# Attention with features: row tiles for the scores, early division of the probabilities, column tiles for the values

## The reference

```python
def _feature_map(x, fm_w, fm_b):
    z = jnp.einsum('nshd,ed->nshe', x, fm_w) + fm_b
    return jnp.concatenate([jnp.exp(z), jnp.exp(-z)], axis=-1)
v, k, q = (_feature_map(x, fm_w, fm_b) for x in (v, k, q))   # 16 heads of 16 -> 32 features
scores = jnp.einsum('nqhd,nkhd->nhqk', q, k) / jnp.sqrt(jnp.float32(EMBED))
attn = jax.nn.softmax(scores, axis=-1)
out = jnp.einsum('nhql,nlhd->nqhd', attn, v)
return out.reshape(N, S, HEADS * EXP_DIM) @ fc_w.T + fc_b
```

## Time and profile before

| | us |
|---|---|
| median of three runs | 1918.85 |
| the profiled execution, its own time | 1920.63 |
| its span | 1918.6 |
| the block that is rewritten (561.9 to 690.3) | 128.4 |
| mean granted clock, share of 2.4 GHz | 0.925 |

### The profile page before, as it was taken

One profiled execution on the slowest core, in us unless ns is written; L12 is line 12 of the kernel. 1 busy time (PEld: TensorE's weight loads), 2 busy tenths in 40 slices (PEclk: granted clock), 3 DMA queues, 4 the chain that ended last, 5 costly groups with the idle time before them and its releaser, 6 DMA issues. The chain is left out here.

```text
span 1918.6 us, 33572 instructions
## 1 busy us (share of the span) xinstructions
PE 1612.3 (84%) x11474; PEld 1174.2 (61%) x11506; DVE 980.2 (51%) x2463; ACT 459.2 (24%) x1027; POOL 399.2 (21%) x651
## 2 busy tenths in 40 slices
PE   4888999999879959699979899376997697999980
PEld 2664888888649943355544555254665463899970
DVE  5454344444476667666646233547885456222223
ACT  1331110111224421355621121242222231111000
POOL 2002111111250001111202343601221201222216
PEclk9999999999889979899989999558998899999995
DMA  3205988989410005334215122300000001899984
GB/s 113 56 2 163 307 298 296 296 303 288 146 55 1 0 1 140 102 99 111 74 30 160 43 82 75 93 6 1 0 0 1 1 2 45 289 322 317 311 251 134
DMA packets 163103, 240.39 MB, mean 125 GB/s; under 512 B 20032, under 2 KB 110464, under 8 KB 162880
## 3 DMA queue, kind: packets, MB, share of 16 engines
q1 hardware_dynamic: 152832, 211.34, 34.3%
q0 software_dynamic: 10176, 27.80, 5.5%
HBM read 208.93 MB, written 30.15 MB: 125 GB/s over the span
## 5 line engine op out<-in xcount | busy, mean ns | idle before, releaser
L1340 DVE TENSOR_REDUCE l1a_nm<-l1a_sc 128x1 f32<-128x512 f32 (+3 forms) x256 | 107.2, 482 | 53.7 <-PE l1a_sc L1476 53.7
L2070 PE MATMUL e0b_gp<-e0b_xT,e0b_wgu 128*128 128x128 f32 x936 | 114.9, 279 | 1.8 <-DVE e0b_hT L2140 1.3
L2070 PEld LDWEIGHTS e0b_gp<-e0b_xT,e0b_wgu 128*128 128x128 f32 x936 | 107.4, 192 | 14.5 <-issue 12.3
L2091 PE MATMUL e0b_yp<-e0b_wd,e0b_hT 128*128 128x256 f32 x468 | 115.1, 388 | 0.6 <-issue 0.6
L2121 ACT ACTIVATE e0b_sg<-e0b_gp 128x640 f32<-128x640 f32 x78 | 33.5, 481 | 285.0 <-PE e0b_gp L2070 285.0
L2091 PEld LDWEIGHTS e0b_yp<-e0b_wd,e0b_hT 128*128 128x128 f32 x468 | 82.6, 189 | 21.9 <-issue 13.9
L2070 PE MATMUL e0b_up<-e0b_xT,e0b_wgu 128*128 128x128 f32 x780 | 93.5, 275 | 0.0
L2070 PEld LDWEIGHTS e0b_up<-e0b_xT,e0b_wgu 128*128 128x128 f32 x780 | 90.2, 192 | 0.0
L2070 PE MATMUL e3b_gp<-e3b_xT,e3b_wgu 128*128 128x128 f32 x624 | 77.4, 277 | 10.1 <-DMA e3b_wgu<-in_L_ffn_W 9.5
L2070 PEld LDWEIGHTS e3b_gp<-e3b_xT,e3b_wgu 128*128 128x128 f32 x624 | 74.5, 192 | 16.5 <-DMA e3b_wgu<-in_L_ffn_W 9.7
L2225 PE MATMUL e1b_gu<-e_kgu,e1b_xT 128*128 x152 | 75.2, 617 | 4.4 <-DVE e1b_xT L2290 2.8
(11 more groups left out here) (576 smaller groups left out, 3566.8 us busy)
## 6 DMA issues: line engine op xcount, KB each, us to landing
e3b_wgu<-in_L_ffn_W SPq DMA_DIRECT2D x78, 512.0 KB, 5.5
e0b_wgu<-in_L_ffn_gate_proj SPq DMA_DIRECT2D x39, 704.0 KB, 4.6
e0b_wgu<-in_L_ffn_up_proj SPq DMA_DIRECT2D x39, 704.0 KB, 6.0
e0b_wd<-in_L_ffn_down_proj SPq DMA_DIRECT2D x39, 640.0 KB, 5.2
e3b_wd<-in_L_ffn_W SPq DMA_DIRECT2D x39, 512.0 KB, 6.6
x_rows<-xn SPq DMA_DIRECT2D x3, 2048.0 KB, 8.6
l_parts<-l1p_split SPq DMA_DIRECT2D x16, 384.0 KB, 3.1
l_stack_k<-l_parts SPq DMA_DIRECT2D x48, 128.0 KB, 2.8
```

Of the source, the lines that this page charges most:

```text
L1340: nc.vector.tensor_reduce(nm[:, g % 2, q, i:i + 1], sc[q], AX_X, ALU.max, negate=True).then_inc(max_done, 1)
L2070: last = nc.tensor.matmul(dst[:, f, :], wgu[j][:, k, at + f * P:at + (f + 1) * P], xT[j][:, k, :], start=(k == 0), stop=(k == KC - 1))
L2091: last = nc.tensor.matmul(yp[:], hT[j][0:FW[f], f, :], wd[j][0:FW[f], f, :], start=(f == 0), stop=(f == FC - 1))
```

## The change

The second block of `feature_attention` is written anew, and the layouts around it follow.

- The features are ordered so that 64 rows hold 2 heads (2 x 2 signs x 16). `fm_signs` is made by quarters of 32, `kd` holds two heads for each half of the rows (`side` in place of `head4`), and `scores` makes two products over 64 rows and 128 columns in place of one over 128 and 256: upper rows into bank `sc[0]`, lower into `sc[1]`.
- `sc` is one tile for all t, no longer two in turn; the transposed probabilities have banks of their own, `pt`.
- Maximum, subtraction and exponentials are done by halves of 8 heads, and `scale` multiplies the probabilities with the reciprocal, by halves, ahead of their transposition. `pr` has AHEAD = 3 buffers.
- `values` has 32 columns of `vd` as the stationary operand and the turned probabilities as the moving one: four products, for four heads, on four column tiles of the array, into the four quarters of the partitions of `ob`. The outputs arise turned; `turn_outputs`, `divide` and `ho` go.
- The bias comes as a product of one row into `yb`; GpSimd's addition goes.
- `w.fc1` is laid out for the new order of heads by eight loads in place of one.
- All loops are written out over t, each queue in an order of its own.

```diff
-    w.fc1, w.bo1 = matrix("L1_xattn_fc_wT", 2 * D, D), spread("L1_xattn_fc_b", D)
+    w.fc1, w.bo1 = sb("w_L1_xattn_fc_wT", [P, 2 * KC, D]), spread("L1_xattn_fc_b", D)
+    for c in range(2 * KC):
+        for half in range(2):
+            at = (c % 2 * 8 + half * 4 + c // 2 * 2) * 2 * HD
+            loads.append((w.fc1[half * P // 2:(half + 1) * P // 2, c, :], ins["L1_xattn_fc_wT"][at:at + P // 2, :]))
...
-                for half, sign in ((slice(0, P // 2), 1.0), (slice(P // 2, P), -1.0)):
+                for quarter in range(4):
+                    rows = slice(quarter * 2 * HD, (quarter + 1) * 2 * HD)
+                    sign = (1.0, -1.0)[quarter % 2]
                     for u in range(2):
-                        nc.vector.tensor_scalar(w.fm_signs[:, u, half], w.fm[:, u * P // 2:(u + 1) * P // 2], sign, None, ALU.mult)
-                    nc.vector.tensor_scalar(w.fmb_signs[half, :], w.fmb[half, :], sign, None, ALU.mult).then_inc(prep, 1)
+                        at = u * P // 2 + quarter // 2 * 2 * HD
+                        nc.vector.tensor_scalar(w.fm_signs[:, u, rows], w.fm[:, at:at + 2 * HD], sign, None, ALU.mult)
+                    nc.vector.tensor_scalar(w.fmb_signs[rows, :], w.fmb[rows, :], sign, None, ALU.mult).then_inc(prep, 1)
...
-                        nc.vector.tensor_tensor(kd[:, b, g], bcast(kT[:, g, b, :], 1, HQ), bcast(const("head4"), 2, L), ALU.mult)
+                        nc.vector.tensor_tensor(kd[:, b, g], bcast(kT[:, g, b, :], 1, 2), bcast(const("side"), 2, L), ALU.mult)
...
+            sc, pt, ob = ([ps(f"{n}{j}", s) for j in range(2)] for n, s in (
+                ("sc", [P, H // 2, L]), ("pt", [P, PAIRS // 2, P]), ("ob", [P, OC, P])))
...
-                    nc.gpsimd.tensor_tensor(x[:], x[:], bcast(bo[:], 1, T), ALU.add).then_inc(biased, 1)
...
+                    def scores(t):
                         pe.wait_ge(q_done, t + 1)
+                        if t >= 1:
+                            pe.wait_ge(less_done, t * 2)
                         for g in range(QC):
+                            for half in range(2):
+                                rows = slice(half * P // 2, (half + 1) * P // 2)
+                                last = nc.tensor.matmul(sc[half][:, g * 2:g * 2 + 2, :].rearrange("p h l -> p (h l)"),
+                                                        qT[rows, t % 2, g, :], kd[rows, t // TB, g].rearrange("p a l -> p (a l)"),
+                                                        start=True, stop=True)
+                                if g == QC - 1:
+                                    last.then_inc(sc_made, 1)
+                    def turn_probs(t):
+                        for half in range(2):
+                            pe.wait_ge(pr_done, t * 2 + half + 1)
+                            if t >= 1:
+                                pe.wait_ge(pt_half, t * 2 + half - 1)
+                            for r in range(half * 4, half * 4 + 4):
+                                last = nc.tensor.transpose(pt[half][:, r % 4, :],
+                                                           pr[t % AHEAD][:, 2 * r:2 * r + 2, :].rearrange("p h l -> p (h l)"), ident)
+                            last.then_inc(pt_made, 1)
+                    def values(t):
+                        if t >= 2:
+                            pe.wait_ge(ot_done, t - 1)
                         for c in range(OC):
+                            if c % 2 == 0:
+                                pe.wait_ge(pt_half, t * 2 + c // 2 + 1)
+                            for i in range(4):
+                                r, a = c * 2 + i // 2, i % 2
+                                pair = r % 4 * 2 + r // 4
+                                last = nc.tensor.matmul(ob[t % 2][i * VD:(i + 1) * VD, c, :], vd[:, t // TB, pair, a, :], pT[:, r, :],
+                                                        start=True, stop=True)
+                        last.then_inc(o_made, 1)
                     def project(t):
...
+                        nc.tensor.matmul(yb[:], ones[0:1, :], bo[0:1, :], start=True, stop=False)
                         for c in range(OC):
+                            last = nc.tensor.matmul(yb[:], hoT[:, c, :], wo[:, c, :], start=False, stop=(c == OC - 1))
...
                     queries(0)
+                    for i in range(T + 3):
+                        if i < T:
+                            scores(i)
+                        if i >= 3:
+                            project(i - 3)
+                        if 2 <= i < T + 2:
+                            turn_probs(i - 2)
+                        if i + 1 < T:
+                            queries(i + 1)
+                        if 2 <= i < T + 2:
+                            values(i - 2)
...
                 def _(act):
...
+                    queries(0)
+                    for i in range(T + 2):
+                        if i < T:
+                            exponentials(i)
+                        if i >= 2:
+                            copy_probs(i - 2)
+                        if i + 1 < T:
+                            queries(i + 1)
+                        if i >= 2:
+                            copy_outputs(i - 2)
...
                 def _(dve):
...
+                    def scale(t):
                         dve.wait_ge(rec_done, t + 1)
+                        for half in range(2):
+                            part = pr[t % AHEAD][:, heads(half), :]
+                            nc.vector.tensor_tensor(part, part, bcast(rs[:, heads(half)], 2, L), ALU.mult).then_inc(pr_done, 1)
...
+                    for i in range(T + 3):
+                        if i < T:
+                            less_maximum(i)
+                        if 1 <= i < T + 1:
+                            sums(i - 1)
+                            scale(i - 1)
+                        if i >= 4:
+                            statistics(i - 4)
+                        if i >= 3:
+                            add(i - 3)
                     statistics(T - 1)
```

More of the change, by code:

```diff
@@ L688, in _, with copy_outputs @@
[L688 to L696 removed]
+                            nc.scalar.copy(pT[:, 4 * half:4 * half + 4, :], pt[half][:]).then_inc(pt_half, 1)
+                    def copy_outputs(t):
+                        act.wait_ge(o_made, t + 1)
+                        if t >= 1:
+                            act.wait_ge(y_made, t)
+                        nc.scalar.copy(hoT[:], ob[t % 2][:]).then_inc(ot_done, 1)
```

179 lines of the change are left out of this document (39 added, 140 removed).

## The result

The changed kernel takes 1910.69 us (median of 20 runs, 1906.32 to 1914.89), the kernel before 1919.26 (20 runs, 1911.91 to 1924.41). The ratio is 0.9958, with a 95% interval of 0.9951 to 0.9965: 8 to 9 us less. The forecast was 13.5 us less and 1905; the measured time lies in the range of 1897 to 1914, at its upper end, and the gain is two thirds of the one forecast. It is real, but falls into the class "within 0.5%", which had been given 0.20, and not into the one that had 0.71.

What follows compares the result with a forecast made beforehand. TensorE's instruction stream was taken as the bound, a tile falling from 7.45 to 6.17 us (6.2 kept). The stage's gain of 13.8 less 0.3 for signs gave 13.5 us, 1905 against 1918.85; range 1897 to 1914.

Steps and rivals of the forecast that it cites:

- within 0.5%: Outcome class for the whole kernel: time within 0.5% (about 9.6 us) of the kernel before, chance 0.20.
- What bounds the kernel: Rewritten attention stage: TensorE's own instruction stream sets the rate, 7.45 us a tile before the change.
- Scores 1.05, values 0.90: TensorE per tile: 16 score products on two row tiles take 1.05 us, 32 value products on four column tiles 0.90.
- Shape changes 0.30, and the bias 0.43: TensorE per tile: changes of the array's shape 0.30 us (bounds 0 and 0.50), two one-row bias products 0.43.
- VectorE 5.86, hand-over chain 5.9: Per tile: VectorE's work sums to 5.86 us; the chain from scores through ScalarE to the next scores takes 5.9.
- the hand-overs bind: Rival: chains between engines, with 0.1 to 0.3 us of slack, set the tile at 6.7 us, total 1911.5; chance 0.17.
- Fill 5.0, 5.0, 6.2: Start of the stage: second and third scores each come 5.0 us after those before, then thirteen steps of 6.2.
- Drain 22: End of the stage: 22 us from the sixteenth scores at 654.5 to the end at 676.5, including 2 for a low clock.
- Signs 0.3: First block's end: twelve small VectorE instructions instead of six for the array of signs cost 0.3 us more.
- Hidden: loads, key patterns, GpSimd's addition, instruction supply: Around the stage: seven more DMA issues, smaller key patterns, GpSimd's dropped addition and written-out loops change nothing, 0.1 us at most.
- The clock in the middle: Rival: TensorE's pauses lower the granted clock for part of the stage, 1945 with half the tiles; chance 0.06.
- the chance of 0.71 for over 0.5%: Outcome class for the whole kernel: faster by over 0.5%, under 1909.3 us, chance 0.71.

Runs made afterwards that it cites:

- e1: Changed kernel with the bias added by GpSimd beside the first tiles, no one-row product on TensorE: tile 5.97 us instead of 6.42, ratio to before 0.9911.
- e3: Changed kernel with the score products issued all upper rows first, then lower, instead of alternating: tile 6.96 us instead of 6.42, ratio to before 0.999.
- e4: Changed kernel with the value products issued column tile by column tile instead of in rotation: tile 7.80 us instead of 6.42, ratio to before 1.007.
- e2: Changed kernel with the bias product over all 128 rows (stationary operand 1/128) instead of one row: tile 6.22 us instead of 6.42, ratio to before 0.990.
- e11: e9 with TensorE doing probabilities and projection before values, and ScalarE's copies before its exponentials: tile 5.79 us, ratio to before 0.9874.
- e7: e1 with the scaling of the probabilities moved from VectorE to GpSimd: tile 5.97 us, as in e1, ratio to before 0.984.
- e8: e6 with eight useless products in each of TensorE's two pauses of the fill: tile 5.97 us, block 109.4 against 110.3, ratio to before 0.9883.
- e10: e9 with the scaling of the probabilities on GpSimd as well: tile 6.19 us, block 110.0, ratio to before 0.9896.
- e12: e11 with the scaling of the probabilities on GpSimd: tile 5.79 us, block 104.7, ratio to before 0.9862.
- e9: e6 with the next queries right behind the scores and their exponential ahead of the tile's: tile 6.19 us instead of 5.97, ratio to before 0.9893.
- e5: Changed kernel with the turning of probabilities 14 and 15 ahead of projections 13 and 14: drain 19.7 us instead of 23.6, ratio to before 0.9907.
- e6: Changed kernel with e1's bias, e5's drain order and the signs made by two VectorE instructions: tile 5.97 us, block 110.3, ratio to before 0.9878.

## Why the prediction was right or wrong

- **What bounds the kernel** (right): TensorE's instruction stream, before and after; no TensorE row of a middle tile shows idle time, and removing one of its products (e1) shortened the tile at once.
- **Scores 1.05, values 0.90** (right, 1.10 and 1.01): the estimates from the first attention's tiles hold, and e3 and e4 show that the gain hangs on the overlap (without that of the rows 0.49 of 1.03 us a tile are left, without that of the columns a tile takes 7.80, more than the 7.45 before). That 1.05 came so near is partly luck: I read the 0.034 of the earlier trace rows as imperfect overlap, but there the second group of four starts 0.213 after the first and every later one 0.112, so the overlap is whole and the difference belongs to the change of shape. By the Trainium skill (TensorE: Matmul & The Clock Gate, Part 3, "What overlaps and what doesn't") a weight load overlaps a running product only where the row group differs, and the four column tiles share it. The trace disagrees: of the 32 weight loads of values each lasts 0.109 and together they take 0.81, four at a time beside running products.
- **Shape changes 0.30, and the bias 0.43** (mechanism right, size wrong; this is the larger part of the miss). The measured tile has 6.42 - (1.05 + 2.15 + 0.87 + 0.90 + 0.90) = 0.55 beyond the products as costed, where 0.30 stood with an upper bound of 0.50. It lies where shapes change: bias + 0.19, projection + 0.11, queries ahead of the column tiles + 0.09, values ahead of the row tiles + 0.11, scores + 0.05. The new order has four changes, and the earlier trace rows priced one at 0.10; I took three, and called those around the bias "perhaps". With the count of changes from the code and the row's price the sum would have been 0.40, and 6.27 a tile. The price was too low as well: the row's 0.10 is what stands before the first product of the new shape, and as much again stands between the first and the second (0.213 for 0.112 in the same scores; e2 measures 0.20 for one whole change). Counted so, the products with whole overlap are 0.87 + 2.15 + 0.87 + 0.90 + 0.87 = 5.66, and 6.42 leaves 0.76, on average 0.19 for each of the four. The same 0.19 gives e2, with three changes, 6.23 (6.22 measured), and the kernels without a bias product, 5.23 and three changes, 5.80 (5.79 in e11). By the Trainium skill (TensorEngine Tiling (Array Packing), Key Properties) changing the tiling mode drains TensorE. The trace agrees in that each change costs, 0.19 and not a whole latency of 0.27; whether it is a drain no run shows. Twelve steps of 6.42 and the third of 6.86 stand where thirteen of 6.2 were forecast: with the first two (9.94 for 10.0) 93.8 from the first scores to the last instead of 90.6, 3.2 of the 4.8 us, 2.6 of them the tile's and most of the rest the clock's in the third step. The other 1.6 are the drain's.
- **VectorE 5.86, hand-over chain 5.9** (right, 5.89 and 5.97). In the changed kernel VectorE works from the maximum at 588.83 to the end of the next add at 594.72, 5.89 us, without idle time; e7 shows the chain bare. The rival "the hand-overs bind" did not happen: 5.97 lies under TensorE's 6.42, and would have under the 6.2 forecast. They bind as soon as TensorE needs less (5.80 in e1 and e7).
- **Fill 5.0, 5.0, 6.2** (two right, third 6.86). I gave the low clock a price at the end, none at the start, though my own chain said that TensorE would pause there: 2.72 and 2.10 us. With the pauses filled (e8) the clock stays at 1.00 and the third step is 6.11, so 6.2 was right at full clock. That the pauses do it is shown for this fill, not in general: e10, e11 and e12 paused 1.57 and 1.54 there and kept 1.00, while e9, with e10's order on TensorE in the fill, did not.
- **Drain 22** (23.6). The step that failed is the order. My list goes from probabilities 14 to values 14 and projection 14 and has no projection 13, which in the code stands between the last scores and probabilities 14; its wait holds both. I read the steady state's order off the code and the drain's off the dependences. At full clock the drain takes 22.0 (e3), where my list gave 20.0; e5, with the probabilities ahead, takes 19.7. I had put 2 us on the low clock; 1.6 is what it cost, and the two errors of size partly cancel.
- **Signs 0.3** (0.8). Twelve small instructions took 1.59 us against 0.74 before. The earlier trace rows price a pair that runs back to back. In the new sequence the first quarter takes 0.24 from start to start and the other three 0.43 to 0.46 (15.38, 15.62, 16.05, 16.51, 16.97); two instructions in place of eight recover 0.6 (e6).
- **Hidden: loads, key patterns, GpSimd's addition, instruction supply** (right). SP waits 68.8 us where it waited 73.2, 4.4 less (seven issues were forecast at 3.3), and nobody waits for it. A key pattern takes 0.26 instead of 0.39.
- **The clock in the middle** (right): 1.00 from 620 to 640 us, with VectorE at 17.83 of 20 us.
- **The whole**: -9.0 + 0.8 = -8.2 by the rows, -8.6 measured. The errors of tile, fill and drain had one sign, each a cost left out; the range held, while the chance of 0.71 for over 0.5% had not allowed for that. I had written that the gain passes 0.5% as long as a tile takes under 6.5 us. At 6.42 it didn't, as the fill and the drain took the rest.

## What to carry to other kernels

Products on tiles of the array overlapped only between near neighbours in TensorE's queue, so let the innermost loop go over the tiles; count the changes of shape in the new order and price each, as a bias of one row was dearer here (a tile of 6.42) than one over all rows (6.22), and both dearer than one that an idle engine adds (5.97). Where a tile's price falls close to other engines' work, write out the loop through single-buffered banks and each engine's queue before moving anything, and ask of each phase which copy it hides (e9). Cost fill and drain from the order that stands in the queues, at both clocks where TensorE pauses, and do not credit an edit with a block's difference before the clocks of the two profiles have been compared (e7, e9, e11).

## What the runs showed of the hardware that I had not expected

- Two pauses of 2.72 and 2.10 us at the start were followed by products at half speed, at a granted clock of 0.81 over 18 us; with products without use in the pauses it was 1.00. In the middle tiles, where TensorE shows no pause, it stayed at 1.00.
- Equal pauses did not always end in a low clock: in the drain, waits of 0.38 and 1.18 us preceded a projection of 3.47 in the changed kernel, waits of 0.57 and 1.19 one of 1.89 in e2.
- A change of the array's shape cost 0.19 us on average, some 0.09 of it before the first product of the new shape and, for the row shapes, 0.10 between the first and the second.
- Column tiles used one after the other cost 0.074 an instruction, between the 0.032 of rotating ones and the 0.109 of full columns: 0.109 on one tile, with the next tile's products starting 0.44 to 0.47 us after this one's first.
- GpSimd multiplies 128 x 512 fp32 by a broadcast in 1.02 us (2.04 for both halves) (e7), and VectorE's add beside it takes 0.40, as without it. VectorE is otherwise nearly idle in that stretch, so whether two large operations disturb each other is not shown.
